# Counting edges in fives of destinations, both visits in one comparison of three, in a GNN and FFN kernel

## The chip, the core and the metric

The kernel runs on one core of a Trainium2 chip. The metric is the device time of one execution in microseconds (us); three runs of the kernel before give a median of 1212.23. All times below are us unless marked ns. The engines are PE (TensorE, with its weight loads as PEld), DVE (VectorE), ACT (ScalarE), POOL (GpSimd) and SP (SyncE, which here only starts transfers).

## The reference

3125 nodes with 256 features go through four residual blocks: a graph convolution of two layers, a feed-forward layer with 8 experts of which 2 are used, a second graph convolution, and a last feed-forward layer with shared and gated experts. Each graph layer takes, for every node, the mean of its neighbours over 103125 edges:

```python
agg = jax.ops.segment_sum(x[src], dst, num_segments=N_NODES)
cnt = jax.ops.segment_sum(jnp.ones((src.shape[0],)), dst, num_segments=N_NODES)
mean = agg / jnp.maximum(cnt, 1.0)[:, None]
return mean @ Wl.T + bl + x @ Wr.T
```

The edges are sorted by `dst`. The kernel makes of them, once, a matrix of counts `adj` (sources by destinations), which all four graph layers then multiply.

## The kernel before, in words

Sources are kept as 25 tiles of 128 (`TILES`), so a source number is a tile number `src >> 7` and a row `src & 127`. Destinations are taken in windows of `W = 6` neighbours: 528 windows (`WINS`), 5 blocks of 128 of them (`WG`). As `dst` is sorted, the edges of a window are one run of the list. The kernel looks at two stretches of 128 edges from the window's first edge on, its two "visits" (`VIS = 2`). An edge of visit `i` that belongs to the window becomes a `key` (place in the window times 25 plus the source's tile) and `low7` (the row).

`first_block` (line 576) is the first stage. On DVE, ACT and PE it normalises x and makes the first dense products, in "quads" of four tiles (`turn`, `y_products`, `z_products`). In between it finds the windows' edges: `tile_numbers` and `first_edges` (790) on DVE give the first edge of each window by a gather of one 128-edge tile of `dst` and a comparison; POOL then gathers `src` and `dst` from there (719 to 724), 256 edges for each window, and `edge_keys` (799) makes keys of them. `first_edges` stands on DVE's queue ahead of `low_parts(0)` and `normalise(2)`, whose rows PE's third `turn` waits for. `fill` and `take_fills` turn the keys round and copy them out; `sum_degrees` (997, product 1006) adds up each destination's edges by 60 one-column products; their inverse goes out by one transfer, and ACT's first eviction of the next stage waits for it (`rows_left`).

`build_counts` (1075) is the count stage. Six windows make a group (`GW`), eight groups a body (`UNROLL`), 11 bodies in all. For each group

- `select` (1164) on DVE compares keys with column numbers (`one_hots`: visit 0 with all 150 columns, visit 1 with the 100 from place 2 on, two instructions of 900 and 600 elements) and rows with 0 to 127 (1536 elements); line 567 is the comparison;
- `count` (1282, product at 1294) on PE multiplies the two for each window: a product of 150 columns and one of 100, the second added to the first, three windows in a PSUM bank;
- `take_counts` (1240, line 1244) on ACT evicts the two banks of the group into `adj` by two instructions.

Between the counts of one body PE does `add_up` (1300, product 1310) for the body before: 98 products of 288 columns (`BW = 8 * 6 * 6`), dealt out in eight shares of 12 or 14. At the end of a body ACT evicts the sums (`take_sums`, 1238) and PE's next share waits for that. Groups have two slots: `select` of a group waits for the count two groups ahead of it, and `count` for the eviction two groups ahead. The counts of body 0 run without `add_up` beside them, the last body's sums without counts.

Of the kernel before, what the change touches and what calls it, by code (L numbers as in the profile page):

```python
# [18 lines left out]
P = 128  # L19
# [11 lines left out]
W = 6  # L31
VIS = 2
WE = VIS * P
WINS = 528
GW = 6
BANKW = 3
# [7 lines left out]
FROM = 2  # L44
# [21 lines left out]

assert W * WINS >= NODES and SSTEPS * SG == ETILES and CHUNKS * CT == TILES
assert BODIES * UNROLL * GW == WINS and UNROLL % SLOT == 0 and NW % 2 == 0 and STMAX % 2 == 0
# [474 lines left out]
assert all(at > UNROLL * GW * W and at + GW * VIS * max(NW, P) <= W * WINS for pair in STAGED_AT.values() for _, at in pair)  # L543


def staged(adj, group):


    (k, at), (low_k, low_at) = STAGED_AT[group]
    sets = GW * VIS  # L550
    return (adj[:, k, at:at + sets * NW].rearrange("p (r n) -> p r n", r=sets),
            adj[:, low_k, low_at:low_at + sets * P].rearrange("p (r n) -> p r n", r=sets))


def one_hots(nc, sel, key, it16):

    for i, first in enumerate(FIRST_OF):
        visits = lambda ap: ap.rearrange("p (w i) n -> p w i n", i=VIS)[:, :, i, :]
        ins = one_hot(nc, visits(sel)[:, :, first:NW], visits(key), it16[:, first:NW], NW - first)
    return ins  # L560
# [12 lines left out]
def first_block(nc, io, g, adj, parts, work):  # L573
# [7 lines left out]
    with ExitStack() as ctx:  # L581
# [34 lines left out]
        edge = take([P, 2, WG], F32)  # L616
# [5 lines left out]
        lo = take([P, 3, WG], F32)  # L622
        over = take([P, VIS * WG + 1], F32)
        bad = take([P, 1], F32)
        idx = take([P, 2, WG], I32)
        gb = take([P, WG, P], I32)
        lower = take([P, WG, P], F32)
        gd = take([P, WG, WE], I32)
        gs = take([P, WG, WE], I32)
        ints = take([P, 2, WG * WE], I32)  # L630
        fl = take([P, 4, WG, WE], F32)
        place = take([P, WINS * VIS], F16)
        here = take([P, W, WINS * VIS], F16)
# [7 lines left out]
        it, it16, ib16 = take([P, NW + TILES + 1], I32), g["it16"], g["ib16"]  # L641
# [11 lines left out]
        LAST_W = WINS - (WG - 1) * P  # L653
# [48 lines left out]
        def _(pool):  # L702
# [3 lines left out]
            nc.gpsimd.iota(it[:, :], pattern=[[1, NW + TILES + 1]], base=0, channel_multiplier=0).then_inc(s["iota_ready"], 1)  # L706
# [7 lines left out]
            for v in range(WG):  # L714
                pool.indirect_dma_start(out=gb[:, v, :], out_offset=None, in_=io["dst"].rearrange("(t e) -> t e", e=P),
                                        in_offset=bass.IndirectOffsetOnAxis(ap=idx[:, 0, v:v + 1], axis=0)
                                        ).then_inc(s["tiles_in"], 16)
            pool.wait_ge(s["idx_ready"], 1)
            for rows, to in ((io["src"], gs), (io["dst"], gd)):
                for v in range(WG):  # L720
                    pool.indirect_dma_start(out=to[:, v, :], out_offset=None,
                                            in_=rows[0:EPAD // WE * WE].rearrange("(t e) -> t e", e=WE),
                                            in_offset=bass.IndirectOffsetOnAxis(ap=idx[:, 1, v:v + 1], axis=1)
                                            ).then_inc(s["gathered"], 16)

        @block.vector
        def _(dve):
# [41 lines left out]
            ch.mark(nc.vector.memset(inverse[:, :, :, :], 1.0))  # L769
# [3 lines left out]
            ch.mark(nc.vector.tensor_scalar(edge[:, 1, :], wp[:, :], -1.0, None, ALU.add))  # L773
            ch.mark(nc.vector.tensor_copy(it16[:, :], it[:, TILES:NW + TILES]))
# [9 lines left out]
            def tile_numbers():  # L784
# [3 lines left out]
                nc.vector.tensor_copy(idx[:, 0, :], lo[:, 0, :]).then_inc(s["tile_ready"], 1)  # L788

            def first_edges():  # L790

                dve.wait_ge(s["tiles_in"], 16 * WG)
                ch.done(nc.vector.tensor_tensor(lower[:, :, :], gb[:, :, :], edge[:, 0, :].unsqueeze(2).broadcast_to([P, WG, P]),
                                                ALU.is_lt))
                ch.done(nc.vector.reduce_sum(lo[:, 1, :], lower[:, :, :], AX.X))
                ch.done(nc.vector.scalar_tensor_tensor(lo[:, 2, :], lo[:, 0, :], float(P), lo[:, 1, :], ALU.mult, ALU.add))
                nc.vector.tensor_copy(idx[:, 1, :], lo[:, 2, :]).then_inc(s["idx_ready"], 1)

            def edge_keys():

                dve.wait_ge(s["gathered"], 16 * 2 * WG)
                src = gs[:, :, :].rearrange("p w e -> p (w e)")
# [3 lines left out]
                ch.done(nc.vector.tensor_tensor(fl[:, 0, :, :], gd[:, :, :], edge[:, 1, :].unsqueeze(2).broadcast_to([P, WG, WE]),  # L806
                                                ALU.subtract))
                ch.done(nc.vector.scalar_tensor_tensor(flat[:, 3, :], flat[:, 0, :], float(TILES), ints[:, 0, :], ALU.mult, ALU.add))
                nc.vector.scalar_tensor_tensor(flat[:, 1, :], flat[:, 0, :], float(W + 1), flat[:, 3, :],
                                               ALU.is_lt, ALU.mult).then_inc(s["fl_ready"], 1)  # L810

            def question():
# [5 lines left out]
                ch.mark(nc.vector.tensor_scalar(over[:, WG:VIS * WG], fl[:, 0, :, P], float(FROM + 1), None, ALU.is_lt))  # L818
                ch.done(nc.vector.tensor_scalar(over[:, 0:WG], fl[:, 0, :, WE - 1], float(W + 1), None, ALU.is_lt))
# [19 lines left out]
            for slot in range(SLOT):  # L839
                at = slice(slot * GW * VIS, (slot + 1) * GW * VIS)  # L840
                ch.mark(one_hots(nc, sel[:, at, :], key[:, at, :], it16))
                ch.mark(one_hot(nc, low[:, at, :], low7[:, at, :], ib16, P))
            low_parts(5)

            def stage(group):
# [3 lines left out]
                ch.mark(one_hots(nc, to, key[:, at, :], it16))  # L849
# [2420 lines left out]
```

## Time and profile before

| | us |
|---|---|
| median of three runs (1211.22 to 1214.56) | 1212.23 |
| span of the profiled execution (first to last instruction) | 1209.0 |
| the median above that span | 3.2 |
| PE busy | 1153.2 (95%) |
| DVE busy | 579.7 (48%) |
| ACT busy | 356.4 (29%) |
| POOL busy | 166.2 (14%) |

The page has no time of the profiled execution beside its span. The span falls into the first stage (to about 77), the counts of body 0 (77 to 91), ten bodies of counts with sums (91.5 to 268.6), the last sums (to 279), and then the layers, which the change does not touch. PE, busy 95% of the span, is the engine to read, but its busy time overlaps itself: a product is listed from its start to the arrival of its last column, so the time a product costs is read from the distance of two starts. The granted clock is a share of TensorE's full 2.4 GHz.

### The profile page before, as it was taken

What the parts mean: (1) busy time and instruction counts of PE and PEld (TensorE: products, weight loads), DVE (VectorE), ACT (ScalarE), POOL (GpSimd) and SP (SyncE); (2) the same over time, 40 slices, a digit from 0 to 9 for tenths busy, and PEclk for the clock granted to TensorE, in tenths of its full rate; (3) what the DMA queues carried; (4) which work ended last, traced back from release to release, by engine and by line L of the source; (5) the groups of instructions that cost most, each with busy time, mean ns of one, the idle gap of its engine ahead of it and who ended that gap; (6) DMA issues with size and microseconds to landing.
All of it is one profiled execution on the core that took longest, in us unless ns stands there. A gap on an engine that the chain in (4) does not pass through costs nothing. (4 is left out here: it accounts for less than half of the span.)

```text
span 1209.0 us, 22437 instructions
## 1 busy us (share of the span) xinstructions
PE 1153.2 (95%) x7928; PEld 879.9 (73%) x7928; DVE 579.7 (48%) x1655; ACT 356.4 (29%) x769; POOL 166.2 (14%) x160
## 2 busy tenths in 40 slices
PE   5979999999999997999999879999999999999998
PEld 4658888886667885888888767555556678876675
DVE  7978888854445668411111164000034445348644
ACT  3464454442220101333333333200012211034333
POOL 4100000000000346444444400000000000001000
PEclk9989999999999998999999989999999999999999
DMA  6610000006653236347765531120046535226101
GB/s 208 178 44 12 22 12 21 22 31 170 179 152 95 93 131 184 85 80 151 148 138 89 97 99 66 62 89 16 31 125 188 147 91 184 77 73 202 44 22 41
DMA packets 134641, 117.83 MB, mean 97 GB/s; under 512 B 23334, under 2 KB 122729, under 8 KB 134560
## 3 DMA queue, kind: packets, MB, share of 16 engines
q1 hardware_dynamic: 104016, 77.67, 22.6%
q0 software_dynamic: 12368, 18.62, 7.9%
q10 hardware_dynamic: 18176, 20.45, 5.0%
q8 instruction: 52, 0.85, 0.3%
q14 instruction: 29, 0.24, 0.1%
HBM read 67.01 MB, written 49.29 MB: 96 GB/s over the span
## 5 line engine op out<-in xcount | busy, mean ns | idle before, releaser
L1310 PE MATMUL b_pa<-adj,l_parts 128*128 (+2 forms) x1078 | 143.5, 284 | 3.7 <-ACT ring L1238 3.7
L1310 PEld LDWEIGHTS b_pa<-adj,l_parts 128*128 128x128 f16 x1078 | 100.8, 98 | 26.6 <-issue 5.5
L2813 POOL DMA_INDIRECT x<-ring,l_ids_now x56 | 87.4, 1561 | 114.1 <-DMA x<-ring,l_ids_now 84.2
L1556 DVE SCALAR_TENSOR_TENSOR l_parts<-dense,scale,l_parts 128x256 f16<-128x256 f32 x48 | 23.2, 484 | 166.0 <-ACT l_parts L1547 165.9
L2630 PE MATMUL l_sum<-l_parts,ring 128*128 128x256 f32 x448 | 101.4, 379 | 0.1
L567 DVE TENSOR_TENSOR ring<-it,key 128x900 f16<-128x900 f16 (+1 forms) x170 | 85.7, 546 | 29.8 <-PE dense L1294 14.1
L1523 PE MATMUL dense<-room,ring 128*128 128x512 f32 x200 | 94.0, 594 | 0.5 <-ACT ring L1504 0.5
L2630 PEld LDWEIGHTS l_sum<-l_parts,ring 128*128 128x128 f32 x448 | 83.0, 190 | 10.5 <-ACT ring L2722 0.3
L2233 PE MATMUL l_sum<-l_parts,adj 128*128 128x256 f16 x735 | 83.0, 273 | 1.3 <-DVE rows L1966 1.2
L2233 PE MATMUL l1b_sum<-l_parts,adj 128*128 128x256 f16 x735 | 82.9, 273 | 0.9 <-DVE rows L1966 0.9
L567 DVE TENSOR_TENSOR room<-ib,low 128x1536 f16<-128x1536 f16 x85 | 80.8, 950 | 0.0
L2233 PEld LDWEIGHTS l_sum<-l_parts,adj 128*128 128x128 f16 x735 | 71.2, 98 | 10.9 <-issue 2.8
L2233 PEld LDWEIGHTS l1b_sum<-l_parts,adj 128*128 128x128 f16 x735 | 71.4, 98 | 10.4 <-issue 2.4
L2760 DVE TENSOR_TENSOR l_ids_now<-l_parts (+1 forms) x28 | 4.5, 161 | 153.6 <-POOLq L2812 148.9
L2218 PEld LDWEIGHTS l_sum<-l_parts,adj 128*128 128x128 f16 x490 | 47.8, 98 | 20.7 <-issue 12.5
L2218 PEld LDWEIGHTS l1b_sum<-l_parts,adj 128*128 128x128 f16 x490 | 47.8, 98 | 20.1 <-issue 12.6
L1244 ACT ACTIVATE adj<-dense 128x450 f32 (+1 forms) x88 | 43.4, 547 | 56.3 <-PE dense L1294 51.0
L2218 PE MATMUL l_sum<-l_parts,adj 128*128 128x256 f16 x490 | 57.4, 273 | 1.5 <-DVE l_parts L1556 0.9
L2218 PE MATMUL l1b_sum<-l_parts,adj 128*128 128x256 f16 x490 | 57.4, 273 | 0.9 <-DVEq L2068 0.6
L482 PE MATMUL n_agg<-adj,l_parts 128*128 128x512 f16 (+2 forms) x294 | 56.3, 351 | 0.0
L1494 DVE SCALAR_TENSOR_TENSOR ring<-ring,unscale 128x256 f32<-128x256 f32 x50 | 23.9, 478 | 65.2 <-DMA ring<-inv 65.1
L1504 ACT ACTIVATE ring<-ring 128x256 f32<-128x256 f32 (+1 forms) x50 | 20.3, 410 | 115.9 <-DVE ring L1496 98.3
(460 smaller groups left out, 1809.1 us busy)
## 6 DMA issues: line engine op xcount, KB each, us to landing
ring<-sums_and_zt SPq DMA_DIRECT2D x50, 256.0 KB, 3.3
l_parts<-in_L_ffn_W SPq DMA_DIRECT2D x16, 512.0 KB, 5.2
l_parts<-slots_in SPq DMA_DIRECT2D x28, 257.0 KB, 3.1
pre<-room ACTq DMA_DIRECT2D x34, 128.0 KB, 2.3
ring<-inv SPq DMA_DIRECT2D x50, 64.0 KB, 4.0
sums_and_zt<-room ACTq DMA_DIRECT2D x5, 640.0 KB, 3.1
adj<-xt SPq DMA_DIRECT2D x5, 640.0 KB, 4.4
adj<-x SPq DMA_DIRECT2D x5, 640.0 KB, 5.6
```

Of the source, the lines that this page charges most:

```text
L482: ins = nc.tensor.matmul(pairs[n % 3][f][:, 0:size], parts[:, k, a, f * P:(f + 1) * P], moving, start=start and a == 0, stop=stop and a == ...
L567: return nc.vector.tensor_tensor(out.rearrange("p r (h two) -> p r h two", two=2), names[:, 0:width].rearrange("p (h two) -> p h two", two ...
L1244: ins = nc.scalar.activation(adj[:, :, ds(group * GW * W + b * BANKW * W, BANKW * W)].rearrange("p k (w j) -> p w k j", j=W), pw[u % SLOT ...
L1310: ins = nc.tensor.matmul(pa[f][:, 0:size], parts[:, k, a, f * P:(f + 1) * P], adj[:, k, ds(r * BW, size)], start=k == 0 and a == 0, stop=k ...
L1494: ch.done(nc.vector.scalar_tensor_tensor(h, h, self.g["unscale"][:, 0:1], self.inv[:, r, :].unsqueeze(1).broadcast_to([P, KD, P]), ALU.mul ...
L1504: return nc.scalar.activation(h, h, ACT.Relu)
L1523: ins = nc.tensor.matmul(self.dense_bank[k % 2][:, :], self.h[:, k % RING, f, :], self.w[:, f, :], start=f == 0, stop=f == KD - 1)
L1556: return nc.vector.scalar_tensor_tensor(parts[:, k, 1, :], bank[:, 0:D], scale, parts[:, k, 0, :], ALU.mult, ALU.subtract)
L2218: ins = nc.tensor.matmul(acc(t), adj[:, k, t * P:(t + 1) * P], parts[:, k, a, :], start=k == 0 and a == 0 and opens(t), stop=k == LAST and ...
L2233: ins = nc.tensor.matmul(acc(t), adj[:, k, t * P:(t + 1) * P], parts[:, k, a, :], start=k == 0 and a == 0 and opens(t), stop=k == LAST and ...
L2630: ins = nc.tensor.matmul(to[t], h[:, n, t * P:(t + 1) * P], w2[:, u, n, :], start=n == 0, stop=n == HB - 1)
L2813: pool.indirect_dma_start(out=g["x1"], in_=y[:, half, t, :], in_offset=None, compute_op=ALU.add, out_offset=bass.IndirectOffsetOnAxis(ap=i ...
```

## The change

Windows are five destinations wide, 640 of them (640 x 5 are the 3200 rows that are stored); eight windows make a group and still eight groups a body: 80 groups in 10 bodies. Each visit is now compared with 75 columns alone (`SPAN = 3` places): visit 0 with places 0 to 2, visit 1 with 2 to 4, in one instruction of 16 sets of 76 columns (one column more than needed, `EVEN_VW`). Visit 1 no longer starts 128 edges after visit 0, but there or at the first edge past place 2, if that comes sooner; edges of `dst` and `src` are stored in pairs, and each visit is gathered by itself. Each window has 128 columns of PSUM; the first product that is written in a bank clears its marks, every other one adds where its columns were written and writes anew where not. ACT evicts a group's 8 x 125 counts by one instruction across two banks. The second slot of row marks is a tile of its own, `lows`, and the scratch area of software transfers is 8 KB of a partition in place of 16. The memsets and transfers for the 32 rows past 528 x 6 are gone.

```diff
-W = 6
+W = 5
-WINS = 528
-GW = 6
-BANKW = 3
+WINS = 640
+GW = 8
+BANKW = 4
-FROM = 2
+SPAN = 3
+FROM = W - SPAN
+VW = SPAN * TILES
+EVEN_VW = VW + VW % 2
...
             for v in range(WG):
-                pool.indirect_dma_start(out=gb[:, v, :], out_offset=None, in_=io["dst"].rearrange("(t e) -> t e", e=P),
+                pool.indirect_dma_start(out=gb[:, v, :], out_offset=None,
+                                        in_=io["dst"][0:EPAD // WE * WE].rearrange("(t e) -> t e", e=WE),
...
-            for rows, to in ((io["src"], gs), (io["dst"], gd)):
+            for i in range(VIS):
                 for v in range(WG):
-                    pool.indirect_dma_start(out=to[:, v, :], out_offset=None,
+                    pool.indirect_dma_start(out=pairs[:, v, i, :], out_offset=None,
...
             def first_edges():
-                ch.done(nc.vector.tensor_tensor(lower[:, :, :], gb[:, :, :], edge[:, 0, :]..., ALU.is_lt))
-                ch.done(nc.vector.reduce_sum(lo[:, 1, :], lower[:, :, :], AX.X))
-                ch.done(nc.vector.scalar_tensor_tensor(lo[:, 2, :], lo[:, 0, :], float(P), lo[:, 1, :], ALU.mult, ALU.add))
-                nc.vector.tensor_copy(idx[:, 1, :], lo[:, 2, :]).then_inc(s["idx_ready"], 1)
+                ch.mark(nc.vector.tensor_tensor(lower[:, :, :], gb[:, :, 0:P], limit(0, P), ALU.is_lt))
+                ch.done(nc.vector.tensor_tensor(under[:, :, :], gb[:, :, :], limit(1, WE), ALU.is_lt))
+                ch.mark(nc.vector.reduce_sum(lo[:, 1, :], lower[:, :, :], AX.X))
+                ch.done(nc.vector.reduce_sum(lo[:, 2, :], under[:, :, :], AX.X))
...
-            for j in range(W):
+            for j in range(SPAN):
                 nc.vector.tensor_scalar(here[:, j, :], place[:, :], float(j + 1), None, ALU.is_equal)...
...
-                one_hots(nc, to, key[:, at, :], it16)
+                one_hot(nc, to, key[:, at, :], it16, EVEN_VW)
...
-                for b in range(HALVES):
-                    ins = nc.scalar.activation(
-                        adj[:, :, ds(group * GW * W + b * BANKW * W, BANKW * W)].rearrange("p k (w j) -> p w k j", j=W),
-                        pw[u % SLOT * HALVES + b][:, 0:BANKW * NW].rearrange("p (w j k) -> p w k j", w=BANKW, j=W), ACT.Copy)
+                counts = pw[u % SLOT][:, :].rearrange("p (w n) -> p w n", w=GW)[:, :, 0:NW]
+                ins = nc.scalar.activation(adj[:, :, ds(group * GW * W, GW * W)].rearrange("p k (w j) -> p w k j", j=W),
+                                           counts.rearrange("p w (j k) -> p w k j", j=W), ACT.Copy)
...
-                        to = pw[u % SLOT * HALVES + w // BANKW][:, w % BANKW * NW + FIRST_OF[i]:(w % BANKW + 1) * NW]
-                        ins = nc.tensor.matmul(to, lows[:, n, :], marks[:, n, FIRST_OF[i]:NW], start=i == 0, stop=i == VIS - 1)
+                        at = w * P + FIRST_OF[i]
+                        ins = nc.tensor.matmul(pw[u % SLOT][:, at:at + VW], lows[:, n, :], marks[:, n, 0:VW],
+                                               start=w % BANKW == 0 and i == 0, stop=w % BANKW == BANKW - 1 and i == VIS - 1,
+                                               skip_group_check=True)
...
-    nc = bacc.Bacc("TRN2", target_bir_lowering=False, num_devices=1)
+    nc = bacc.Bacc("TRN2", target_bir_lowering=False, num_devices=1, dynamic_dma_scratch_size=8192)
```

On PE in the loop over bodies, one count and the share of sums behind it, before. `dense` and `b_pw` are the two slots' PSUM, `ring` and `room` hold the marks:

```order
L1294 MATMUL dense<-ring,room 128x150 [waits b_copied,b_sel_ready]
L1294 MATMUL dense<-ring,room 128x100
...
L1310 ISA
L1310 MATMUL b_pa<-adj,l_parts 128x288 x4
...
L1287 REGISTER_ALU
L1294 MATMUL b_pw<-ring,room 128x150 [waits b_copied,b_sel_ready]
```

The same place now:

```order
L1291 MATMUL dense<-ring,room 128x75 [waits b_copied,b_sel_ready]
L1291 MATMUL dense<-ring,room 128x75 x15
L1309 ISA
L1309 MATMUL b_pa<-adj,l_parts 128x320 x4
...
L1284 REGISTER_ALU
L1291 MATMUL b_pw<-ring,lows 128x75 [waits b_copied,b_sel_ready]
```

A count is 16 products of 75 columns in place of six of 150 and six of 100, and a share of sums still 12 or 14 products, of 320 columns in place of 288; the waits are the same.

On DVE in the first stage, `first_edges` with the step behind it, before:

```order
L793 TENSOR_TENSOR adj<-adj 128x640 [waits n1_tiles_in,n1_scales_done]
L795 TENSOR_REDUCE adj<-adj 128x5 [waits n1_vector_chain]
L796 SCALAR_TENSOR_TENSOR adj<-adj 128x5 [waits n1_vector_chain]
L797 CAST adj<-adj 128x5 [waits n1_vector_chain]
L763 SCALAR_TENSOR_TENSOR l_parts<-n_y,scale,l_parts 128x2x256 [waits n1_high_done] x2
```

The same place now:

```order
L791 TENSOR_TENSOR adj<-adj 128x640 [waits n1_tiles_in,n1_scales_done]
L792 TENSOR_TENSOR adj<-adj 128x1280
L793 TENSOR_REDUCE adj<-adj 128x5 [waits n1_vector_chain]
L794 TENSOR_REDUCE adj<-adj 128x5
L795 SCALAR_TENSOR_TENSOR adj<-adj 128x5 [waits n1_vector_chain]
L796 SCALAR_TENSOR_TENSOR adj<-adj 128x5
L797 SCALAR_TENSOR_TENSOR adj<-adj 128x5 [waits n1_vector_chain]
L798 TENSOR_SCALAR adj<-adj 128x10 [waits n1_vector_chain]
L760 SCALAR_TENSOR_TENSOR l_parts<-n_y,scale,l_parts 128x2x256 [waits n1_high_done] x2
```

Four instructions became eight ahead of the same step, one of them a comparison and one a sum over 256 edges in place of 128. The names are all `adj` because the first stage keeps its tables in that tile's space.

## Rows read from the trace of the kernel before

**Rows 1.** The page's first line.

```profile
span 1209.0 us, 22437 instructions
```

**Rows 2.** Busy by stretch: length, PE, PEld, DVE, ACT, POOL; clock, DMA share, GB/s.

```profile
30.00:60.00 30.00, 29.01 (x119) 19.81 (x120) 28.73 (x87) 14.77 (x24) 4.95 (x6) 1.00 0.62 181
77.40:91.40 14.00, 10.42 (x119) 9.17 (x120) 12.22 (x21) 8.56 (x18) 1.05 (x4) 0.74 0.06 9
109.40:127.20 17.80, 17.47 (x195) 14.89 (x196) 15.03 (x25) 8.61 (x19) 0.00 (x0) 1.00 0.05 19
```

**Rows 3.** Timeline of the count loop: start, us, engine, instruction, [idle before <-releaser].

```profile
131.79 1.01 DVE L567 TENSOR_TENSOR ring<-it,key 128x900 f16<-128x900 f16 x2 [0.25 <-PE b_pw L1294]
132.72 0.95 DVE L567 TENSOR_TENSOR room<-ib,low 128x1536 f16<-128x1536 f16 x1
132.93 0.82 PE L1294 MATMUL dense<-ring,room 128*128 128x150 f16 x12
133.59 1.63 PE L1310 MATMUL b_pa<-adj,l_parts 128*128 x12
...
135.06 0.82 PE L1294 MATMUL b_pw<-ring,room 128*128 128x150 f16 x12
...
143.82 0.82 PE L1294 MATMUL b_pw<-ring,room 128*128 128x150 f16 x12
144.11 0.71 ACT L1238 ACTIVATE ring<-b_pa 128x288 f32<-128x288 f32 x2 [0.71 <-PE b_pa L1310]
...
144.96 1.64 PE L1310 MATMUL b_pa<-adj,l_parts 128*128 x12 [0.32 <-ACT ring L1238]
...
161.88 0.71 ACT L1238 ACTIVATE ring<-b_pa 128x288 f32<-128x288 f32 x2 [0.71 <-PE b_pa L1310]
```

**Rows 4.** Groups by form, 91.4 to 269.3: busy, mean ns, idle and releasers.

```profile
L567 DVE TENSOR_TENSOR room<-ib,low 128x1536 f16<-128x1536 f16 x78 | 74.1, 951 | 0.0
L567 DVE TENSOR_TENSOR ring<-it,key 128x900 f16<-128x900 f16 x77 | 48.4, 629 | 26.0 <-PE dense L1294 14.1 <-PE b_pw L1294 11.9
L567 DVE TENSOR_TENSOR ring<-it,key 128x600 f16<-128x600 f16 x77 | 35.7, 464 | 0.0
...
L1244 ACT ACTIVATE adj<-dense 128x450 f32 x72 | 35.5, 547 | 45.1 <-PE dense L1294 45.1
...
L1238 ACT ACTIVATE ring<-b_pa 128x288 f32<-128x288 f32 x20 | 7.1, 408 | 8.6 <-PE b_pa L1310 8.6
```

**Rows 5.** Timeline, the products of `sum_degrees`.

```profile
73.98 1.75 PE L1006 MATMUL n_few<-adj 128*128 128x1 f16 x60
```

**Rows 6.** Timeline, the first stage around `first_edges`, and the first one-hots.

```profile
21.85 0.82 DVE L793 TENSOR_TENSOR adj<-adj 128x640 f32<-128x640 int32 x1
...
22.71 0.82 DVE L795 TENSOR_REDUCE adj<-adj 128x5 f32<-128x640 f32 x1
...
24.37 1.41 DVE L763 SCALAR_TENSOR_TENSOR l_parts<-n_y,scale,l_parts 128x512 f16<-128x512 f32 x2 [0.44 <-ACT l_parts L895]
...
30.99 1.09 PE L956 MATMUL dense<-ident,adj 128*128 128x128 f32 x8 [1.03 <-DVE adj L737]
...
62.28 1.01 DVE L567 TENSOR_TENSOR ring<-it,key 128x900 f16<-128x900 f16 x2 [2.12 <-ACT low L909]
```

**Rows 7.** Groups by form on DVE, 0 to 77.4.

```profile
L806 DVE TENSOR_TENSOR adj<-adj 128x1280 f32<-128x1280 int32 x1 | 1.5, 1481 | 0.0
...
L817 DVE TENSOR_REDUCE adj<-adj 128x1 f32<-128x896 f32 x1 | 1.1, 1087 | 0.0
```

**Rows 8.** Busy by stretch, columns as in rows 2, in the counts of body 0.

```profile
84.90:88.30 3.40, 1.65 (x24) 1.34 (x24) 3.40 (x7) 2.57 (x6) 0.00 (x0) 1.00 0.02 5
88.40:91.70 3.30, 2.83 (x25) 2.55 (x26) 3.30 (x6) 1.09 (x3) 0.00 (x0) 0.50 0.05 11
```

**Rows 9.** Timeline, DVE in the counts of body 0.

```profile
86.51 1.00 DVE L567 TENSOR_TENSOR ring<-it,key 128x900 f16<-128x900 f16 x2
...
88.30 1.00 DVE L567 TENSOR_TENSOR ring<-it,key 128x900 f16<-128x900 f16 x2
```

More of the change, by code:

```diff
@@ L542 @@
 STAGED_AT = {2: ((14, 640), (15, 640)), 3: ((16, 640), (17, 640)), 4: ((18, 640), (12, 640))}
-assert all(at > UNROLL * GW * W and at + GW * VIS * max(NW, P) <= W * WINS for pair in STAGED_AT.values() for _, at in pair)
+assert all(at > UNROLL * GW * W and at + GW * VIS * P <= ROWS for pair in STAGED_AT.values() for _, at in pair)
 def staged(adj, group):
@@ L550, in staged @@
     sets = GW * VIS
-    return (adj[:, k, at:at + sets * NW].rearrange("p (r n) -> p r n", r=sets),
+    return (adj[:, k, at:at + sets * EVEN_VW].rearrange("p (r n) -> p r n", r=sets),
             adj[:, low_k, low_at:low_at + sets * P].rearrange("p (r n) -> p r n", r=sets))
[L555 to L560, printed above, removed]
 def one_hot(nc, out, values, names, width):
@@ L615, in first_block @@
         wlo = take([P, WG * P], F32)
-        edge = take([P, 2, WG], F32)
+        edge = take([P, 4, WG], F32)
         first = take([P, EG], F32)
@@ L848, in stage @@
                 to, low_to = staged(adj, group)
[L849 removed]
+                ch.mark(one_hot(nc, to, key[:, at, :], it16, EVEN_VW))
                 ch.mark(one_hot(nc, low_to, low7[:, at, :], ib16, P))
@@ L1105, in build_counts @@
         gc, ghi = split(scratch("low7", 3 * NW, I32), 3), scratch("low7", NW, F16)
-        hib = sel[:, 0:2, :].rearrange("p r n -> p (r n)")[:, 0:BW]
-        HALVES = GW // BANKW
-        pw = work.dense_bank + [pr.ps(f"b_pw{i}", [P, 512]) for i in range(AHEAD, SLOT * HALVES)]
+        hib = work.ring[:, 0:BW // 2].bitcast(F16)
+        general = work.ring[:, 0:SG * EVEN_NW // 2].bitcast(F16).rearrange("p (r n) -> p r n", r=SG)
+        pw = [work.dense_pair] + [pr.ps(f"b_pw{i}", [P, GW * P]) for i in range(1, SLOT)]
         pa = [pr.ps(f"b_pa{f}", [P, BW]) for f in range(KD)]
@@ L1284, in count @@
                 ahead, slot = isinstance(group, int) and group in STAGED, slice(u % SLOT * GW * VIS, (u % SLOT + 1) * GW * VIS)
-                marks, lows = staged(adj, group) if ahead else (sel[:, slot, :], low[:, slot, :])
+                marks, lows = staged(adj, group) if ahead else (sel[:, slot, :], low[u % SLOT])
                 if not isinstance(group, int) or group >= SLOT + len(STAGED_AHEAD):
@@ L1319, in _ @@
             with pe.If(flag != 0):
-                pe.wait_ge(s["ready"], 4)
+                pe.wait_ge(s["ready"], 2)
                 with pe.Fori(0, WINS) as v:
@@ L1365, in _ @@
             flag = sp.value_load(g["flag"][0:1, 0:1])
-            sp.wait_ge(s["ready"], 4)
-            sp.dma_start(g["sums"][:, :, NWIN:ROWS], sums[:, :, 0:ROWS - NWIN]).then_inc(s["rest_out"], 16)
             def load_ahead():
@@ L3209, in program @@
         parts = held.enter_context(nc.sbuf_tensor("l_parts", [P, TILES, 2, D], F16))
-        dense_bank = [held.enter_context(nc.psum_tensor(f"dense{i}", [P, 512], F32)) for i in range(AHEAD)]
-        work = Work(nc, io, g, room, ring, parts, dense_bank)
+        dense = held.enter_context(nc.psum_tensor("dense", [P, AHEAD * 512], F32))
+        dense_bank = [dense[:, i * 512:(i + 1) * 512] for i in range(AHEAD)]
         with ExitStack() as keys:
+            lows = keys.enter_context(nc.sbuf_tensor("lows", [P, GW * VIS, P], F16))
+            work = Work(nc, io, g, room, ring, parts, dense, dense_bank, lows)
             for name in ("key", "low7"):
                 g[name] = keys.enter_context(nc.sbuf_tensor(name, [P, WINS * VIS, 2], F16))
-            for name, size in (("it16", NW), ("ib16", P)):
+            for name, size in (("it16", EVEN_NW), ("ib16", P)):
                 g[name] = keys.enter_context(nc.sbuf_tensor(name, [P, size], F16))
@@ L3252, in layout @@
     arrays["dst"] = padded(arrays["dst"], EPAD, FAR)
+    arrays["edges"] = np.ascontiguousarray(np.stack([arrays["dst"], arrays["src"]], axis=1).reshape(-1))
     for n in GNN_WEIGHTS:
```

121 lines of the change are left out of this document (59 added, 62 removed).

## The prediction

> **What bounds the kernel now.** The first view is busy time by stretch. In a body of the count loop PE is busy 17.47 of 17.80 us at the full clock, DVE 15.03, ACT 8.61; between 30 and 60 PE is busy 29.01 of 30 and DVE 28.73 [rows 2]. So the count loop is PE's, and the first stage belongs to PE and DVE together. The timeline confirms it: in the loop DVE waits 0.25 for PE in each group, ACT waits for PE, and PE waits only at the end of a body, 0.32 for ACT's eviction of the sums [rows 3, 4]. What DVE or ACT save in the loop is worth nothing by itself; what counts is the time between starts of PE's products.
>
> **What a product costs.** From the start of a count to the start of the sums behind it are 133.59 - 132.93 = 0.66 for 12 products of together 1500 columns; from there to the next count 135.06 - 133.59 = 1.47 for 12 products of 288 [rows 3]. At 2.4 columns per ns these are 0.625 and 1.44, so a product costs its columns plus 2.5 to 2.9 ns, though each has its own weights. Is there a floor that 75 columns would meet? The 60 one-column products of the degrees take 1.75 from the first start to the last end; less one duration of about 0.17 that is 1.58 over 59 steps, 27 ns for a product with a weight load of the same shape [rows 5]. A product of 75 columns takes 31.3 + 2.9 = 34 ns, above that floor. The bounds are 31 ns (columns alone) and 44 ns (what a product of 100 columns costs now, 41.7 + 2.9, if a narrower one were no shorter); I take 34, since both neighbours follow columns.
>
> The Trainium skill, "TensorE: Matmul & The Clock Gate", section Back-to-back issue gap, speaks against this: in a stream of weight loads and products it gives about 81 ns per product at 128 columns, so narrow products should not pay. By that 16 products would be an estimated 1.3 us, and a body some 6 us longer than I say. The trace does not agree: products of 150 and 100 columns together cost 110 ns here, 55 each [rows 3].
>
> **The loop, before and after.** A body lasts 161.88 - 144.11 = 17.77 [rows 3]: 98 x 122.5 ns = 12.00 for the sums, 8 x 0.66 = 5.28 for the counts, and 0.49 at its end, where PE's next sums start at 144.96 although its count, started at 143.82, was through 0.66 later. Ten bodies, the last without its eighth count, are 177.0. After: sums 98 x (320/2.4 + 2.5 = 135.8 ns) = 13.31; counts 128 x 34.2 ns = 4.37; the end of a body 0.64 (0.49, plus 0.11 because the count that lies beside ACT's work is shorter, plus 0.05 because two evictions of 320 columns take 32 more each at 0.83 ns). Together 18.32, nine of them less one count 164.3. **The loop gives 12.7.** The columns of the sums are the same in all, 98 times the stored destinations; the gain is 96,000 columns of counts in place of 132,000, less the fixed 2.9 ns of 224 more products. The last sums keep their 246 columns.
>
> Can DVE and ACT follow? The three forms of the comparison give a line: 464 ns at 600 elements, 629 at 900, 951 at 1536, so 0.51 to 0.55 ns per element [rows 4]. 1216 elements make 0.79, 2048 make 1.21; an instruction starts about 0.08 before the end of the one ahead of it (132.72 against 131.79 + 1.01), so a group costs 1.84 after 1.79 now (88.30 - 86.51) [rows 3, 9]. PE's shortest step is 12 x 0.1358 + 0.55 = 2.18, so DVE keeps 0.34 of slack, now 0.25 plus the waits at a body's end. ACT's 450 columns take 547 and 288 take 408 ns [rows 4], 0.86 ns per column with 0.16 fixed, so 1000 columns take about 1.0, as the two instructions together now. If reading across two banks cost something, ACT would have 1 us per group to spend before PE waits. These three cost nothing, covered by PE.
>
> **The first stage.** `first_edges` becomes longer. Now 21.85 to 23.93 (24.37 less DVE's wait of 0.44 for ACT) [rows 6]. After: comparisons 0.82 and 1.48, sums 0.82 and 1.49 (from 1.09 at 896 elements), each second one starting 0.08 early, four small ones of 0.17 to 0.2 with their waits: 5.2 for 2.1. Less the 0.44, normalise(2) is 2.7 later. PE waits for it already, 1.03 before its transposes at 30.99 [rows 6], and has no gap from there to 60 in which to catch up [rows 2], so the 2.7 go through to the end of the stage. That is nothing only if PE's wait were hidden, and no row suggests it. The later steps have cover: the gathers are as many as before, start 3 later and are needed some 20 later; the strided key arithmetic may lose up to 1.5 on DVE, which waits 2.12 for ACT ahead of its first marks [rows 6].
>
> PE's wait becomes 1.03 + 2.7 = 3.7 long. In the counts of body 0 the clock was halved after a stretch in which PE was busy 1.65 of 3.40, and the next 3.30 ran at 0.50 [rows 8]. A gap of 3.7 with nothing in it should do at least that. 3.4 us of work at half the clock cost 1.7. Bounds 0 (no fall) and 3.4 (twice as long); I take 1.7.
>
> Given back: the degrees need 30 products in place of 60, 30 x 27 ns = 0.8, and DVE merges two small instructions into one, 0.1; ACT's first eviction waits for the inverse, so both count. Three of the six comparisons ahead of them go, hidden behind PE's turning of the keys. ACT's last copies of keys are wider (640 windows for 528), 0 to 0.4, taken as 0.1. Body 0's counts have three comparisons of DVE in a row before its first sums, 3 x 0.05 = 0.15, and evictions that last as long as before.
>
> The smaller scratch area of POOL's transfers has no price in the trace: POOL's indirect transfers come in bursts of ten or fewer behind waits for other engines, so I take 0; up to 2 if a burst were held up. Memsets and one transfer that go were beside other work.
>
> **Sum.** -12.7 + 2.7 + 1.7 - 0.9 + 0.1 + 0.15 = -8.9, with -4 and -12 as its ends (start worse by 5; no fall of the clock and the first edges half hidden). From the span of 1209.0 [rows 1] that is 1200.1; the runs' median lies 3.2 above the span, so 1203.3.
>
> **Rivals.** (a) Narrow products are no shorter than those of 100 columns: 10 ns more for 1152 products in the loop, 11.5, gives 1215. For it: nothing between 1 and 100 columns is in the trace. Against: the one-column floor of 27 ns. It decides from 42 ns per product (8.9/1152 = 7.7 ns above mine), where the change is worth nothing, and past 45 it is slower. This is the case on the other side.
> (b) DVE becomes the bound: 76 columns in one instruction run at the rate of the 1280-element comparison of 32-bit numbers, 1481 ns [rows 7], so 1216 take 1.42 and a group 2.47. Against PE's mean step of 18.32/8 = 2.29 that is 0.18 for 72 groups, 13, giving 1216. Against it: the 600, 900 and 1536 forms, two of them rows of 100 and 150 in a strided place, lie on one line.
> (c) The start costs about double, 9 in place of 4, by a longer half-clock or by the wider gather of 1 KB rows landing after DVE is ready: 1208.
> (d) The start costs next to nothing, as PE's clock holds and DVE overlaps its sums: 1200.
> (e) Two-bank evictions or the shared PSUM marks make PE wait in each group, so that a step stays at 2.3: 72 x 0.1 = 7, giving 1210. ACT's 1 us of slack speaks against it.
>
> **Chances.** Forecast with (d) 0.77; (c) 0.09; (e) 0.04; (a) 0.06; (b) 0.04. A measurement of this kernel can tell about 0.3%, 3.6 us, from no change: below 1208.6 is faster, above 1215.8 slower. Half of (c) and most of (e) fall between them, half of (a) and (b) above. Faster 0.82, same 0.11, slower 0.07. The forecast's own range is 1200 to 1208. Holding the time 8 times in 10, the range reaches to 1198 (products at their bound of 31 ns take 3.5 off, beside part of (d)) and to 1209 (c).
>
> **What would show it.** A body (from one eviction of the sums to the next) of 18.3, with 0.55 from the start of a count to the start of its sums; 0.65 or more there is rival (a). A wait of DVE for PE in each group of 0.3; PE waiting for DVE is (b). The two new sums and comparisons around 22 to 27, PE's third transposes near 33.7, the clock at 0.50 for some 3 us behind them, and ACT's first eviction of counts some 3.5 later than before. A loop shorter by less than 9, or a start later by more than 9, would make the forecast wrong.

## The result, and the profile after

The changed kernel takes 1204.05 us (median; 1202.8 to 1204.77) where the kernel before takes 1212.24: a ratio of 0.993, with a 95% interval of 0.9917 to 0.9942. The forecast was 1203.3. The direction and the size are right; of the terms, two are right, two were mis-sized, one came in some executions only, and one was missing. The profiled execution:

```profile
span 1201.3 us, 22170 instructions
```

The count loop comes first. The timeline of the changed kernel around the end of a body and the two groups behind it answers to [rows 3]:

```profile
114.54 0.72 PE L1291 MATMUL b_pw<-ring,lows 128*128 128x75 f16 x16
114.83 0.77 ACT L1239 ACTIVATE ring<-b_pa 128x320 f32<-128x320 f32 x2 [0.58 <-PE b_pa L1309]
...
115.74 1.80 PE L1309 MATMUL b_pa<-adj,l_parts 128*128 x12 [0.47 <-ACT ring L1239]
...
117.38 0.73 PE L1291 MATMUL dense<-ring,room 128*128 128x75 f16 x16
...
117.94 1.79 PE L1309 MATMUL b_pa<-adj,l_parts 128*128 x12
118.26 1.30 ACT L1245 ACTIVATE adj<-dense 128x1000 f32 x1 [1.47 <-PE dense L1291]
118.27 0.79 DVE L563 TENSOR_TENSOR ring<-it,key 128x1216 f16<-128x1216 f16 x1 [0.91 <-PE dense L1291]
118.98 1.22 DVE L563 TENSOR_TENSOR room<-ib,low 128x2048 f16<-128x2048 f16 x1
...
119.57 0.72 PE L1291 MATMUL b_pw<-ring,lows 128*128 128x75 f16 x16
...
133.28 0.77 ACT L1239 ACTIVATE ring<-b_pa 128x320 f32<-128x320 f32 x2 [0.59 <-PE b_pa L1309]
```

From the start of a count to its sums are now 117.94 - 117.38 = 0.56 (before 0.66, for six windows instead of eight), from there to the next count 1.63, and a body lasts 133.28 - 114.83 = 18.45. The end of a body costs 115.74 - 114.54 = 1.20 in place of 0.56, so 0.64, as forecast. PE still sets the pace. The groups by form between 94.9 and 260 answer to [rows 4] and show the two engines beside it:

```profile
L563 DVE TENSOR_TENSOR ring<-it,key 128x1216 f16<-128x1216 f16 x69 | 54.7, 792 | 27.4 <-PE dense L1291 15.9 <-PE b_pw L1291 11.5
L563 DVE TENSOR_TENSOR lows<-ib,low 128x2048 f16<-128x2048 f16 x35 | 42.7, 1219 | 0.0
...
L1245 ACT ACTIVATE adj<-dense 128x1000 f32 x32 | 41.6, 1301 | 34.6 <-PE dense L1291 34.6
```

DVE has the forecast 0.79 and 1.22 and waits for PE. ACT's eviction takes 1.30 where 1.0 was forecast, and still waits 34.6 / 32 = 1.1 for PE each time.

Now the way to the loop: the timeline of the changed kernel at the steps of [rows 5, 6], then at ACT's first evictions, the first sums and the last sums:

```profile
21.88 0.82 DVE L791 TENSOR_TENSOR adj<-adj 128x640 f32<-128x640 int32 x1
...
22.63 1.48 DVE L792 TENSOR_TENSOR adj<-adj 128x1280 f32<-128x1280 int32 x1
...
24.88 1.47 DVE L794 TENSOR_REDUCE adj<-adj 128x5 f32<-128x1280 f32 x1
...
26.94 1.41 DVE L760 SCALAR_TENSOR_TENSOR l_parts<-n_y,scale,l_parts 128x512 f16<-128x512 f32 x2
...
33.45 1.09 PE L961 MATMUL dense<-ident,adj 128*128 128x128 f32 x8 [2.90 <-DVE adj L734]
...
64.73 0.79 DVE L563 TENSOR_TENSOR ring<-it,key 128x1216 f16<-128x1216 f16 x1 [1.88 <-ACT low L914]
...
76.65 0.89 PE L1011 MATMUL n_few<-adj 128*128 128x1 f16 x30
...
81.76 1.29 ACT L1245 ACTIVATE adj<-dense 128x1000 f16<-128x1000 f32 x1 [4.31 <-DMA inv<-adj]
82.94 1.29 ACT L1245 ACTIVATE adj<-b_pw 128x1000 f16<-128x1000 f32 x1
...
94.89 3.40 PE L1309 MATMUL b_pa<-adj,l_parts 128*128 x12
...
262.66 10.45 PE L1309 MATMUL b_pa<-adj,l_parts 128*128 128x246 f16 x98 [0.95 <-ACT ring L1239]
```

The same four late places in the kernel before:

```profile
79.49 0.98 ACT L1244 ACTIVATE adj<-dense 128x450 f16<-128x450 f32 x2 [5.09 <-DMA inv<-adj]
80.36 1.00 ACT L1244 ACTIVATE adj<-b_pw 128x450 f16<-128x450 f32 x2
...
91.53 1.74 PE L1310 MATMUL b_pa<-adj,l_parts 128*128 x12
...
268.63 10.45 PE L1310 MATMUL b_pa<-adj,l_parts 128*128 128x246 f16 x98 [0.89 <-ACT ring L1238]
```

Read in pairs, the third transposes are 2.46 later, the first one-hots 2.45, the end of the degrees 1.81 (77.54 after 75.73), the first eviction 2.27, the first sums 3.36. From the first to the last sums are 167.77 in place of 177.10; these 9.33 are close to the 9 below which the prediction called itself wrong. What follows takes 938.6 in place of 940.4, although no work in it changed. The stretches of the changed kernel (length, busy time of PE, PEld, DVE, ACT, POOL, then the granted clock, DMA share, GB/s):

```profile
34.00:37.40 3.40, 3.40 (x13) 1.73 (x12) 3.23 (x14) 1.77 (x3) 2.49 (x4) 1.00 0.45 117
79.50:89.60 10.10, 7.70 (x110) 6.73 (x106) 6.83 (x8) 7.40 (x6) 0.20 (x2) 0.50 0.02 2
93.10:99.80 6.70, 5.90 (x47) 4.27 (x48) 4.66 (x6) 2.59 (x3) 0.00 (x0) 0.50 0.03 6
114.83:133.28 18.45, 17.98 (x232) 14.11 (x229) 15.42 (x17) 11.06 (x11) 0.00 (x0) 1.00 0.06 20
...
478.80:482.10 3.30, 3.11 (x19) 2.63 (x18) 0.76 (x5) 1.96 (x5) 2.48 (x3) 1.00 0.52 172
```

The clock did not fall behind the third transposes, where the forecast had it; it was at half from 93.1 to 99.8, over the first sums, where the forecast had full clock. That raised the questions for the experiments: are narrow products priced by columns, does the longer `first_edges` really pass through, what does the clock follow, and why did the eviction and body 0 grow?

### The profile page after: what moved, and what is told of

The parts are those of the page before. It is cut to its first block and busy times, and to the rows that moved or that the text cites. A ratio compares the mean times of both kernels' runs of the same rounds, so it can differ in the third digit from the quotient of the medians.

```text
span 1201.3 us, 22170 instructions
## 1 busy us (share of the span) xinstructions
PE 1140.6 (95%) x8024; PEld 857.3 (71%) x8024; DVE 571.3 (48%) x1553; ACT 373.3 (31%) x671; POOL 165.4 (14%) x158
## 5 line engine op out<-in xcount | busy, mean ns | idle before, releaser
L1309 PEld LDWEIGHTS b_pa<-adj,l_parts 128*128 128x128 f16 x980 | 91.8, 98 | 36.0 <-issue 6.0
L2226 PEld LDWEIGHTS l1b_sum<-l_parts,adj 128*128 128x128 f16 x735 | 71.4, 98 | 10.4 <-issue 2.4
L563 DVE TENSOR_TENSOR ring<-it,key 128x1216 f16<-128x1216 f16 x77 | 61.0, 792 | 32.5 <-PE dense L1291 15.9
L1245 ACT ACTIVATE adj<-dense 128x1000 f32 (+1 forms) x40 | 52.0, 1299 | 43.1 <-PE dense L1291 38.7
L1245 ACT ACTIVATE adj<-b_pw 128x1000 f32 (+1 forms) x40 | 51.9, 1299 | 25.5 <-PE b_pw L1291 25.5
```

The lines of the kernel that those rows point to most:

```text
L563: return nc.vector.tensor_tensor(out.rearrange("p r (h two) -> p r h two", two=2), names[:, 0:width].rearrange("p (h two) -> p h two", two ...
L1245: ins = nc.scalar.activation(adj[:, :, ds(group * GW * W, GW * W)].rearrange("p k (w j) -> p w k j", j=W), counts.rearrange("p w (j k) -> ...
L1309: ins = nc.tensor.matmul(pa[f][:, 0:size], parts[:, k, a, f * P:(f + 1) * P], adj[:, k, ds(r * BW, size)], start=k == 0 and a == 0, stop=k ...
L2226: ins = nc.tensor.matmul(acc(t), adj[:, k, t * P:(t + 1) * P], parts[:, k, a, :], start=k == 0 and a == 0 and opens(t), stop=k == LAST and ...
```

## Experiments

Ratios are to the kernel before, measured beside each, with 95% intervals. Where a span is compared, it ends at the last sums' start, since the layers behind add differences of their own.

**Wider and narrower products.** Every count product with 100 columns, and in the loop with 25:

```diff
-nc.tensor.matmul(pw[u % SLOT][:, at:at + VW], lows[:, n, :], marks[:, n, 0:VW], ...)
+nc.tensor.matmul(pw[u % SLOT][:, at:at + 100], lows[:, n, :], flat[:, from_:from_ + 100], ...)   # e1
+nc.tensor.matmul(pw[u % SLOT][:, at:at + 25], lows[:, n, :], marks[:, n, 0:25], ...)             # e2
```

> Every count product has 100 columns in place of 75 (it reads 25 columns of the next set and writes them in its own window, so the counts are not the reference's); number of products, waits, comparisons and evictions stay. If a product costs its columns at 2.4 per ns plus 3 to 4 ns, it takes 45 ns in place of 35.3, a count 0.72 in place of 0.56, a body 18.45 + 8 x 0.16 = 19.7, and nine bodies make the kernel about 11 us slower than the changed kernel: 1215. Rival: 35 ns is a floor set by the weight load and not by columns; then 100 columns may hide in it in part and the body stays below 19.2.

> In the loop over bodies every count product has 25 columns in place of 75 (most counts are left out); the rest stays. If columns alone set the price, a product takes 13 ns and a count 0.21; the group's step then is 1.63 + 0.21 = 1.84 and DVE, at 1.84 to 1.9 a group, becomes the bound. If there is a floor near the 27 ns of the one-column products, a count takes 0.43 and a body 18.45 - 8 x 0.13 = 17.4, about 9 us off the changed kernel (1195). If the 35.3 ns of now are already the floor, count and body stay at 0.56 and 18.45, and the time at 1204.

Ratios 1.0003 (0.9991 to 1.0015) and 0.9854 (0.9837 to 0.9871). One count and its sums, first with 100 and then with 25 columns:

```profile
137.79 0.87 PE L1292 MATMUL dense<-ring,room 128*128 128x100 f16 x16
138.50 1.79 PE L1310 MATMUL b_pa<-adj,l_parts 128*128 x12
```

```profile
150.07 0.55 PE L1291 MATMUL dense<-ring,room 128*128 128x25 f16 x16
150.47 1.79 PE L1309 MATMUL b_pa<-adj,l_parts 128*128 x12
```

A count takes 0.71, 0.56 and 0.40 for 100, 75 and 25 columns: 44, 35 and 25 ns a product. Columns at 2.4 per ns are 41.7, 31.3 and 10.4. So the price is columns plus 2.5 to 4 ns until a floor of 25 ns, and 75 columns lie above it. The Trainium skill, "TensorE: Matmul & The Clock Gate", section Back-to-back issue gap, has both: its formula for isolated products and its floor agree with these rows within 2 ns; its 81 ns for streams of weight loads and products at 128 columns does not fit them, though no run has products of 128. Bodies are 19.46 and 17.33 long (175.07 - 155.61 and 165.76 - 148.43), so nine of them explain the 9 lost and the 10 won. The whole gain hangs on this: with products of 100 columns the kernel is as fast as before.

**Without the second edge.** The comparison and sum over 256 edges and one of the four small instructions are gone (the expectation says two), and visit 1 always starts 128 edges after visit 0:

```diff
-ch.done(nc.vector.tensor_tensor(under[:, :, :], gb[:, :, :], limit(1, WE), ALU.is_lt))
-ch.done(nc.vector.reduce_sum(lo[:, 2, :], under[:, :, :], AX.X))
-... at_edge[:, 2, :] and the ALU.min with it
+ch.done(nc.vector.tensor_scalar(at_edge[:, 1, :], at_edge[:, 0, :], float(P), None, ALU.add))
```

> The second comparison and the second sum of the first edges and two small instructions are gone; the second visit always starts 128 edges after the first, so that some edges are missed. My account: the price of the longer first edges reaches the end in full. DVE's next step can then start at 24.9, when ACT's parts are there, in place of 26.94: PE's third transposes are 2.0 to 2.3 earlier (31.3), the first one-hots too, and the time falls by 2 to 2.5 to about 1202. Rival: the price is hidden by a later wait or given back by the clock: third transposes earlier but the time within 0.7 of the changed kernel's.

```profile
30.71 1.09 PE L958 MATMUL dense<-ident,adj 128*128 128x128 f32 x8 [0.96 <-DVE adj L734]
```

PE's third transposes come 2.74 earlier, back where they were before the change [rows 6]. The first one-hots start at 61.99, the first sums at 91.54, and the last sums 4.2 earlier than in the changed kernel: within the count stages the price is confirmed, and more than it comes back. The time as a whole, 1209.01 (0.9975, 0.9965 to 0.9986), missed the expectation. From the last sums on this kernel takes 949.4, 10 to 11 longer than the two profiles of the changed kernel, and it runs 22295 instructions in place of 22170. Its counts lack edges, so the layers work on other numbers; that other tokens then go to other experts is the likely reason, argued and not shown.

**Made twice.** The second comparison and its sum once more, in the same place:

```diff
+ch.done(nc.vector.tensor_tensor(under[:, :, :], gb[:, :, :], limit(1, WE), ALU.is_lt))
+ch.done(nc.vector.reduce_sum(lo[:, 2, :], under[:, :, :], AX.X))
```

> The second comparison and the second sum of the first edges are made twice, 2.9 to 3.1 more on DVE in the same place; PE's wait ahead of its third transposes becomes about 5.9. As the prediction had it, this passes through in full and such a gap halves the clock for one stretch behind it: third transposes at 36.5, half clock behind them, in sum 3 to 4.7 slower than the changed kernel of this call. Rival 1: passes through, but the clock holds: 3 slower. Rival 2: what DVE loses there is not on the path to the end: less than 1.5 slower.

```profile
36.59 1.09 PE L963 MATMUL dense<-ident,adj 128*128 128x128 f32 x8 [2.44 <-DVE adj L734]
```

Against the first profile it passes through to the third transposes (3.1) and the first one-hots (67.87, 3.1), but the last sums start at 263.51, only 0.8 later. The time, 1205.82 (0.9953, 0.9939 to 0.9966), is 2.1 above the changed kernel measured beside it: less than any form of my account, more than the second rival, and the two intervals overlap at their rims. Its clock was at half from 31.5 to 34.8, but over products behind which PE waited 2.44 for DVE all the same, so that this cost nothing.

**Sums later.** The two sums and the small instructions stand behind `normalise(2)`:

```diff
 first_edges()          # the two comparisons alone
 low_parts(0)
 normalise(2)
+edge_sums()
 low_parts(1)
```

> The two sums over edges and the four small instructions behind them stand behind the normalising of the third chunk, in place of ahead of it; the work is the same. The gathers start some 6 later, at about 33, and are needed at 53. If PE sets the pace from its third transposes on (as the prediction had it), these start at 31.3 in place of 33.45 and the time falls by about 2 to 1202. If DVE does, which in the changed kernel has no gap from 32 to 62.7, the first one-hots stay at 64.7 and the time at 1204, within 0.5.

```profile
31.68 1.09 PE L966 MATMUL dense<-ident,adj 128*128 128x128 f32 x8 [0.81 <-DVE adj L734]
...
40.83 1.09 PE L966 MATMUL dense<-ident,adj 128*128 128x128 f32 x8 [1.17 <-DVE adj L734]
```

Neither theory. The third transposes are 1.8 earlier, but the next ones that wait for DVE wait 1.17, which the changed kernel doesn't have; the first one-hots come 0.4 earlier, the first eviction 1.0, at 80.72. Both engines are close to the pace between 30 and 60: of the 1.8 that PE gets, 0.4 is left once DVE has had its turn. The ratio, 0.992 (0.9908 to 0.9933), is not told apart from the changed kernel's.

**The inverse in a tile of its own**, so that ACT's first eviction needn't wait for its transfer:

```diff
-inverse = take([P, 2, WG, W], F32)
+inverse = g["inverse"]      # a tile beside adj
-rows_left(act)
+act.wait_ge(g["zt_out"], 16 * len(QUADS))
```

> The table of inverse degrees lies in a tile of its own and no longer in the counts' space, so ACT's first eviction waits only for the first count (and the transfers that are through by then). My account: the chain from the inverse's transfer over ACT to PE sets the counts of body 0. ACT's first eviction starts near 80.3 in place of 81.76, the first sums near 93.5 in place of 94.9, and the time falls by 1.4, beside what the clock does. Rival: DVE's comparisons or the halved clock set body 0, and the first sums stay at 94.9.

```profile
80.55 1.29 ACT L1245 ACTIVATE adj<-dense 128x1000 f16<-128x1000 f32 x1 [3.08 <-PE dense L1291]
```

As expected in the trace: ACT now waits for PE, the first eviction is 1.2 and the first sums (93.25) 1.6 earlier than in the first profile. The first eviction varies by itself, though: it is at 81.4 and 81.3 in the profiles of the next two versions, which are unedited up to there. By the ratio, 0.9935 (0.992 to 0.995), no gain can be told.

**Two evictions**, one for each bank:

```diff
+for b in range(0, GW, BANKW):
+    ins = nc.scalar.activation(adj[:, :, ds(group * GW * W + b * W, BANKW * W)]..., counts[:, b:b + BANKW, :]..., ACT.Copy)
```

> ACT evicts the counts of a group by two instructions of 500 columns, one for each bank, in place of one of 1000. If it is the reach across two banks that made the eviction 1.29 in place of the 1.0 that was forecast, each takes 0.59 (as 450 columns took 0.547), and two of them about 1.07. If it is the form (five neighbours in place of six, or 25 tiles by eight windows), each takes about 0.7 and two of them 1.35 to 1.4. In the loop ACT has 0.9 of idle time in a group, so that the body stays at 18.45 either way; body 0 changes by less than 1 and the time by less than 1.

```profile
L1246 ACT ACTIVATE adj<-dense 128x500 f32 x64 | 41.6, 730 | 33.9 <-PE dense L1292 33.9
```

One of 500 columns takes 730 ns, where 450 took 547 [rows 4], and a pair of them 1.30, as long as the one of 1000. So reaching across two banks costs nothing; the new form (five neighbours for each tile and window) costs more per column. The Trainium skill, "ScalarE: Activation LUTs", section What ACT_TABLE_LOAD costs, gives 186 ns and 0.833 ns an element, which would make 1000 columns an estimated 1.02; the old form and the sums agree with it (547 and 408 ns for 450 and 288), the new one does not. Which property of the form does it was not tried. Ratio 0.9928 (0.9912 to 0.9945): no change.

**Keeping PE busy.** Four products of 320 columns, into a bank that nobody reads, behind each of the last four counts of body 0:

```diff
 count(0, u)
+for _ in range(4 if u >= 4 else 0):
+    nc.tensor.matmul(pd[:, :], parts[:, 0, 0, 0:P], ..., start=True, stop=True)
```

> Behind each of the last four counts of body 0 PE does four further products of 320 columns into a bank that nobody reads. If the halved clock at the start of the loop (93.1 to 99.9 in the changed kernel) comes from PE's idle time in body 0, the clock is back at full before the first sums, their first share takes 1.8 in place of 3.4, and the loop gives 2 to 2.5 more; the counts of body 0 may come up to 1 later by the added work, so the time falls by 1 to 2.5. Rival: the halving does not follow PE's idle time here; then the windows of half clock stay where they are and the time rises by 0 to 1.5.

```profile
87.50:94.20 6.70, 4.59 (x85) 3.49 (x84) 6.02 (x7) 5.39 (x5) 0.00 (x0) 1.00 0.03 9
94.30:97.70 3.40, 3.40 (x22) 2.13 (x20) 3.15 (x4) 1.29 (x1) 0.00 (x0) 0.50 0.02 5
```

Not as expected: the half clock began 1.2 later than in the first profile, at 94.3, but still lay on the first share of the sums, which took 3.30 and not 1.8. It was half as long, and from the first to the last sums the time was 166.9 in place of 167.8; but the unedited kernel's second profile, below, has 3.4 at half and 166.7 without any added product, so nothing of this can be put down to them. PE had no added work behind the first count of body 1 and stood idle for 1.18 there. Ratio 0.9919 (0.9904 to 0.9933): no gain can be told.

**Scratch.** The kernel before with 8 KB:

```diff
-nc = bacc.Bacc("TRN2", target_bir_lowering=False, num_devices=1)
+nc = bacc.Bacc("TRN2", target_bir_lowering=False, num_devices=1, dynamic_dma_scratch_size=8192)
```

> The kernel before with a scratch area of 8 KB for software transfers in place of 16, as in the changed kernel. Taken as free: the same time, within 0.7. Rival: bursts of ten indirect transfers are held up, in the first stage and in the layers with experts: up to 2 slower.

Ratio 1.0003 (0.999 to 1.0015): free, as forecast.

**The changed kernel again**, unedited:

> The changed kernel unedited, with a second profile beside the ones it is compared with. Its first profile had the clock at half from 93.1 to 99.9 and, in the layers, for 10.2 from 468.5 in place of the 13.7 of all other profiles. If both are chances of one execution and not of the kernel, this one ends its counts at 271.5 to 273.5, its layers take 929.5 to 930.5 in place of 928.4, and the ratio to before stays at 0.993. If the shorter halving in the layers belongs to the change, it is there again.

Ratio 0.9931 (0.9918 to 0.9945). The second profile at the places of the first, from the third transposes to the last sums, then three stretches:

```profile
33.55 1.64 PE L962 MATMUL dense<-ident,adj 128*128 128x128 f32 x8 [3.46 <-DVE adj L735]
...
66.52 0.79 DVE L564 TENSOR_TENSOR ring<-it,key 128x1216 f16<-128x1216 f16 x1 [3.55 <-ACT low L915]
...
78.44 0.89 PE L1012 MATMUL n_few<-adj 128*128 128x1 f16 x30
...
83.48 1.29 ACT L1246 ACTIVATE adj<-dense 128x1000 f16<-128x1000 f32 x1 [4.24 <-DMA inv<-adj]
...
96.01 3.16 PE L1310 MATMUL b_pa<-adj,l_parts 128*128 x12
...
262.71 10.45 PE L1310 MATMUL b_pa<-adj,l_parts 128*128 128x246 f16 x98 [0.95 <-ACT ring L1240]
```

```profile
34.00:37.30 3.30, 3.30 (x9) 2.00 (x8) 3.16 (x13) 1.19 (x2) 2.55 (x3) 0.50 0.44 119
81.80:88.50 6.70, 4.30 (x64) 3.81 (x60) 4.78 (x5) 4.91 (x4) 0.00 (x0) 0.50 0.02 4
...
478.80:481.00 2.20, 2.20 (x7) 1.75 (x6) 0.00 (x0) 0.48 (x1) 1.64 (x2) 0.50 0.72 240
```

The same kernel now has the clock at half behind its third transposes, after a wait of 3.46 where the first profile shows 2.90, and its first one-hots are 1.8 and its first eviction 1.7 later. Seven profiles are of kernels unedited up to there: these two and those with 100 and 25 columns, the inverse apart, two evictions and PE kept busy. Three of them have the half clock there, each behind a wait of 3.46; four, behind waits of 2.30 to 2.96, have not. At the start of the sums the clock is then at half for 3.4 only, and from the first to the last sums are 166.70. The layers have the longer half clock, past 478.8, that the kernel before has too, and take 939.5. In the other versions, that without the second edge aside, they take 939.1 to 940.7, in the kernel before 940.4 and with 8 KB 940.8. So the 1.7 that the layers seemed to gain in the first profile is not told apart from chance.

**Two edits together, and all three.** Sums later with the inverse apart; and then also four added products behind each of the last three counts of body 0 and behind the first of body 1:

```diff
 count(0, u)
+if u >= 5:
+    keep_busy()
...
 count(1, 0)
+keep_busy()
```

> The sums over edges behind the normalising of the third chunk and the inverse table in a tile of its own, together. Each alone brought the first eviction 1.0 to 1.2 earlier. If they act at two different places (DVE's order, ACT's wait) they add: first eviction near 79.4, first sums near 92.3, and the time 2 to 3 below the changed kernel of this call. Rival: both remove the same wait, and the time is that of one of them, about 1 below.

> The two edits together with four further products of 320 columns on PE behind the last three counts of body 0 and behind the first count of body 1. If the halved clock at the start of the sums comes from PE's idle time ahead of them, it is at full there: the first share of sums takes 1.8 in place of 3.3, and the time is 1 to 2 below that with the two edits alone. Rival: the halving comes whatever PE does there; then the first share stays at 3.3 and the time is the same or up to 0.5 longer.

With two edits the first eviction is at 79.50 and the first sums at 92.63: in these profiles the two add, as my account had it. The ratio is 0.992 (0.9906 to 0.9934), and by the medians it gains 1.5 on the changed kernel, with intervals that overlap; in this profile the clock was at half from 79.7 to 96.6. With all three:

```profile
86.40:90.80 4.40, 3.77 (x62) 2.65 (x60) 4.40 (x6) 3.69 (x4) 0.00 (x0) 1.00 0.01 4
92.16:97.00 4.84, 4.84 (x65) 3.81 (x62) 4.84 (x6) 2.75 (x3) 0.00 (x0) 1.00 0.02 3
```

```profile
92.16 1.79 PE L1319 MATMUL b_pa<-adj,l_parts 128*128 x12
...
257.51 10.45 PE L1319 MATMUL b_pa<-adj,l_parts 128*128 128x246 f16 x98 [0.95 <-ACT ring L1244]
```

The first share takes 1.79, the loop 165.35, and the kernel 1198.66: a ratio of 0.9895 (0.988 to 0.991), 5.1 below the changed kernel measured beside it (0.9931, 0.9918 to 0.9945), with intervals apart. This version beats both. The added products' own share is 3.6 by the medians; the intervals with and without them overlap at their rims (0.9906 and 0.991). In the two profiles 2.4 of it is there at the last sums (257.51 after 259.92), and the rest lies in the layers, where nothing was changed.

## Why the prediction was right, step by step

| step | forecast | first profile | second profile |
|---|---|---|---|
| `first_edges`, to the third transposes | +2.7 | +2.46 | +2.56 |
| clock behind them, to the first one-hots | +1.7 | -0.01 | +1.68 |
| copies and degrees, to the degrees' end | -0.8 | -0.64 | -0.64 |
| inverse's transfer, to the first eviction | 0 | +0.46 | +0.39 |
| body 0, to the first sums | +0.15 | +1.09 | +0.49 |
| loop at full clock (from the version with all three) | -12.7 | -11.75 | -11.75 |
| clock at the start of the loop | 0 | +2.42 | +1.35 |
| layers | 0 | -1.73 | -0.88 |
| sum | -8.9 | -7.7 | -6.8 |

- **Products by columns** held; the loop's term was mis-sized by 1, since a product of 75 columns costs 35.3 ns and not 34.2. Nine bodies of 8 x 16 of them make 1.2. Rival (a) is excluded by the 25 columns, which go down to 25 ns.
- **DVE and ACT follow** held for DVE to 0.01. For ACT the price was wrong (1.30 for 1.0), the cover right: it still waits for PE in every group. Rivals (b) and (e) are out.
- **`first_edges` passes through** held as far as the first one-hots, shown from both sides: 2.74 earlier without the second edge, 3.1 later with two of them. How much of it reaches the end is not shown: at the last sums the one is 4.2 earlier and the other 0.8 later, and the steps between differ by 1 to 2 from profile to profile without any such edit, as the table shows. The reason was only half of it: not PE alone sets the pace there, but PE and DVE by turns.
- **The clock at the third transposes** was the right mechanism and size, but came in three of seven profiles, where the wait was 3.46, and not behind 2.30 to 2.96; the forecast had a wait of 3.7. It should have given the fall a chance, not its full 1.7.
- **The degrees' products** gave 0.86 (0.89 for 1.75), as forecast. The steps between the first one-hots and them took 0.22 more, where 0.1 was forecast.
- **The inverse's transfer** is scatter: from the degrees' end to the first eviction are 3.76 in the kernel before and 4.22 and 4.15 in the two profiles, but 3.5 to 3.7 in the versions with 100 columns, 25 columns, two evictions and PE kept busy, which leave it as it is.
- **Body 0** was mis-sized: evictions start every 1.18 (82.94 - 81.76) where a group's two started every 0.87, and "evictions that last as long as before" was wrong where nothing covers it. Counts at half clock take 1.2, and the half clock lay on body 0 for 10.1 in the first profile and 6.7 in the second. No experiment parts the two.
- **The clock at the start of the loop** is the missing term: the kernel before had its half clock just ahead of the sums [rows 8], the changed one has it on them. PE has less to do in a group of body 0 (0.56 for 0.66 at full clock) and waits longer for evictions; that this moved the fall is argued. That PE's idle time decides rests on one version: with products behind every count from the sixth of body 0 to the first of body 1, the first share took 1.79 in its one profile, where it takes 2.8 to 3.4 in the other eleven profiles of kernels with five destinations. The version with one gap left open does not add to it.

The start as a whole (first sums 3.36 and 4.48 later, for a forecast of 3.75) is neither rival (c), 9, nor rival (d), next to nothing.

So the forecast's closeness, 0.8, is in part luck: in the first profile what it missed (+2.4, +0.5, +0.9, +1.0 and +0.2 on the degrees) stands against what didn't come (-1.7), a shorter `first_edges` (-0.2) and the layers' -1.73, a chance of one profile. The runs' median fell by 8.2, the interval allows 7.0 to 10.1, and the two profiles of the changed kernel lie 7.7 and 6.8 below the one of before.

## What to carry to other kernels

Price a matmul from the distance of two starts in the same loop, not from its listed duration, and then find the floor: here narrow products pay by columns down to about 25 ns, so it was worth comparing less and multiplying more often. A step that makes PE idle costs its length, and then, in some executions, a stretch at half clock behind it; a few products into an unused bank behind each count ahead of the loop bought back more than moving the step did, while with one gap left open no gain could be told. An engine's price that is hidden in the loop can be paid in the loop's first body, where the engine is not hidden. And one profile is one execution: before a difference of 1 or 2 is put down to an edit, a second profile of the unedited kernel shows how much comes by chance.

## What the runs showed of the hardware

- Products of 25, 75, 100 and 320 columns with a new weight load each cost 25, 35, 44 and 136 ns from start to start.
- An eviction of 1000 columns across two PSUM banks costs the same 1.30 as two of 500 in one bank each; the form with five neighbours costs 730 ns at 500 columns, the one with six 547 at 450.
- The same program had the clock at half behind a wait of 3.46 and at full behind one of 2.90 in the same place; over seven profiles it was at half behind 3.46 (three) and at full behind 2.30 to 2.96 (four). The Trainium skill, "TensorE: Matmul & The Clock Gate", section What's actually happening, says that the point at which the clock rises at the start of a kernel varies from run to run; the two profiles show such a difference at a fall within one.
